# AdaLN attention and FFN in one kernel: the order of the first tiles' statistics on GpSimd and ScalarE, and who splits W_out

## What is computed

```python
mod = (_silu(L0_c) @ L0_wmod).reshape(B, 6, 1, -1)
sa, ca, ga, sb, cb, gb = (mod[:, i] for i in range(6))
ga, gb = ((2 * (g >= 0) - 1) * jnp.maximum(jnp.abs(g), 0.25) for g in (ga, gb))
h = _layernorm(x) * (1 + ca) + sa
x = x + ga * attn(h)      # Xn = layernorm(h)*gamma+beta; Q,K,V = Xn @ W_in + b_in; rotary on K, V
                          # A = 0.5 * sum over rows of cos_sim(K)*cos_sim(V) + 0.5
                          # (A * Q) @ W_out + b_out + h
h = _layernorm(x) * (1 + cb) + sb
x = x + gb * ffn(h)       # relu(h @ W_up.T) @ W_down.T + sum(softmax(top2 logits)) * (h @ W_expert)
```

## Time and profile before

| | us |
|---|---|
| median of 3 executions | 382.82 (381.12 to 384.11) |
| the profiled execution, its own time | 382.15 |
| its span, first to last instruction | 380.1 |
| PE busy in the span | 358.8 (94%) |
| DVE busy | 252.9 (67%) |
| ACT busy | 169.2 (45%) |
| POOL busy | 126.0 (33%) |

### The profile page before, as it was taken

How to read it: one execution, slowest core, us unless ns; L and a number is a source line. 1 busy time by engine, 2 the same in 40 slices (tenths; PEclk the granted TensorE clock), 3 DMA queues, 4 the chain that set the end, 5 groups by cost and what they waited for, 6 DMA issues and landing times.

```text
span 380.1 us, 4613 instructions
## 1 busy us (share of the span) xinstructions
PE 358.8 (94%) x1632; PEld 281.3 (74%) x1632; DVE 252.9 (67%) x510; ACT 169.2 (45%) x307; POOL 126.0 (33%) x127
## 2 busy tenths in 40 slices
PE   4879798999998999989999999999999999999996
PEld 1237286788886888868888878888788878877885
DVE  2788979857978588785988459718550845184354
ACT  1477776773347711375116672156125512541210
POOL 0186746984932439225362142900010001000000
PEclk9989899989999999999999999999999999999999
DMA  6978457430030000000000003001100110011003
GB/s 195 390 310 321 206 223 245 161 93 2 1 83 0 2 0 30 0 1 0 2 28 2 0 0 112 28 0 55 58 3 0 55 57 0 0 59 54 0 2 111
DMA packets 10967, 27.43 MB, mean 72 GB/s; under 512 B 1200, under 2 KB 1584, under 8 KB 9792
## 3 DMA queue, kind: packets, MB, share of 16 engines
q1 hardware_dynamic: 10944, 27.13, 19.7%
HBM read 22.90 MB, written 4.23 MB: 71 GB/s over the span
## 4 chain that ended last, share of the span: by engine, by line
PE 71%; issue 9%; DVE 7%; DMA 4%; ACT 4%; POOL 3%; SPq 1%; DVEq 0%; POOLq 0%; ACTq 0%
PE ps L1144 22%; PE ps L1146 21%; PE ps L1145 21%; DMA stage<-in_wmod 3%; PE ps L1192 2%; DMA xs<-in_X 2%; PE ps L1169 1%; ACT sqj L498 1%; ACT ps L561 1%; POOL hrs L358 1%; POOL w_lo L361 1%; PE ps L1302 1%; PE ps L1303 1%; ACT t_hi L563 1%; DVE hb L735 1%
## 5 line engine op out<-in xcount | busy, mean ns | idle before, releaser
L1144 PE MATMUL ps<-w_hi,t_hi 128*128 128x512 f32 x192 | 76.4, 398 | 0.3 <-POOL w_lo L361 0.3
L1146 PE MATMUL ps<-w_hi,t_lo 128*128 128x512 f32 x192 | 75.5, 393 | 0.0
L1145 PE MATMUL ps<-w_lo,t_hi 128*128 128x512 f32 x192 | 75.3, 392 | 0.0
L1144 PE MATMUL ps<-t_hi,w_hi 128*128 128x512 f32 x128 | 51.2, 400 | 1.4 <-DVE sb_col L1012 1.4
L1144 PE MATMUL ps<-w_hi,g_hi 128*128 128x512 f32 (+1 forms) x132 | 51.3, 389 | 0.0
L1146 PE MATMUL ps<-w_hi,g_lo 128*128 128x512 f32 (+1 forms) x132 | 50.6, 383 | 0.0
L1145 PE MATMUL ps<-w_lo,g_hi 128*128 128x512 f32 (+1 forms) x132 | 50.5, 383 | 0.0
L1146 PE MATMUL ps<-t_hi,w_lo 128*128 128x512 f32 x128 | 50.0, 391 | 0.0
L1145 PE MATMUL ps<-t_lo,w_hi 128*128 128x512 f32 x128 | 49.9, 390 | 0.0
L1144 PEld LDWEIGHTS ps<-w_hi,t_hi 128*128 128x128 f32 x192 | 36.5, 190 | 10.0 <-DVE t_lo L762 1.1
L1146 PEld LDWEIGHTS ps<-w_hi,t_lo 128*128 128x128 f32 x192 | 36.3, 189 | 7.8
(11 more groups left out here) (148 smaller groups left out, 641.4 us busy)
## 6 DMA issues: line engine op xcount, KB each, us to landing
stage<-in_w SPq DMA_DIRECT2D x4, 1024.0 KB, 6.1
out<-xs SPq DMA_DIRECT2D x15, 256.0 KB, 2.0
xs<-in_X SPq DMA_DIRECT2D x3, 1024.0 KB, 9.0
xs<-in_wmod SPq DMA_DIRECT2D x8, 256.0 KB, 6.1
stage<-in_w SPq DMA_DIRECT2D x8, 256.0 KB, 8.5
stage<-in_wmod SPq DMA_DIRECT2D x2, 1024.0 KB, 9.3
gate_bc<-mod_rows SPq DMA_DIRECT2D x8, 256.0 KB, 3.3
xs<-in_X SPq DMA_DIRECT2D x2, 512.0 KB, 6.9
```

The source lines that it names most:

```text
L1144: mm(dst, l_hi, r_hi, start=start, stop=False)
L1145: mm(dst, l_hi, r_lo, start=False, stop=False)
L1146: return mm(dst, l_lo, r_hi, start=False, stop=stop)
```

## The change

On POOL, `rstd_x0(1)` moves behind tile 0's `shift_h0`. On PE, `mod_pair` runs all four chunks ahead of the transposes of tile 0, and the transposes of tile 1 move from before chunk 1 to before chunk 2 of `kv_tile(0,0)`. On ACT, the copy of the scale and shift rows moves from behind the last cast of W_V to a place ahead of tile 0's `t0_evac`, and the cast of W_K's last chunk moves behind tile 1's `normalise`. POOL only casts W_out, four chunks in a row ahead of `rstd_x(2)` and `weight(0,3)`; DVE makes the four low parts behind the last `t_split` of batch 0's turn.

```diff
@@ gpsimd
                 nc.gpsimd.tensor_copy(w_hi[:, WO, k, :], raw).then_inc(whi_out, 1)
-                pool.wait_ge(whi_out, k + 1)
-                nc.gpsimd.tensor_tensor(w_lo[:, WO, k, :], raw, w_hi[:, WO, k, :].bitcast(f32), ALU.subtract).then_inc(wlo_out, 1)
...
                     rstd_h(1, 2, 2)
-                    out_weight(0)
+                    for k in range(NC):
+                        out_weight(k)
                     rstd_x(2)
-                    out_weight(1)
                     weight(b, 3)
-                    out_weight(2)
-                    out_weight(3)
...
             rstd_x0(0)
-            rstd_x0(1)
             low_kv(0, 0)
             shift_h0(0)
+            rstd_x0(1)
             low_kv(1, 0)
@@ scalar
             normalise(0, 0, 1)
             split_hi_kv(1, 2)
-            split_hi_kv(0, 3)
+            act.wait_ge(mod_ps, 1)
+            nc.scalar.activation(rows, ps[0:64, MOD_BANK, :], ACT.Identity, bias=row_bias, scale=half[0:64, 0:1]).then_inc(mod_sb, 1)
             t0_evac(0)
             normalise(0, 1, 1)
+            split_hi_kv(0, 3)
             split_hi_kv(1, 3)
-            act.wait_ge(mod_ps, 1)
-            nc.scalar.activation(rows, ps[0:64, MOD_BANK, :], ACT.Identity, bias=row_bias, scale=half[0:64, 0:1]).then_inc(mod_sb, 1)
             normalise(0, 2, 1)
@@ vector
+            def split_lo_out(k):
+
+                dve.wait_ge(whi_out, k + 1)
+                v.tensor_tensor(w_lo[:, WO, k, :], w_raw[3][:, k * D:(k + 1) * D],
+                                w_hi[:, WO, k, :].bitcast(f32), ALU.subtract).then_inc(wlo_out, 1)
...
                 t_split(1, 2)
                 t_split(1, 3)
+                for k in range(NC):
+                    split_lo_out(k)
@@ tensor
-            def mod_pair(ks):
-                for k in ks:
+            def mod_pair():
+                for k in range(NC):
...
-                if ks[-1] == NC - 1:
-                    last.then_inc(mod_ps, 1)
+                last.then_inc(mod_ps, 1)
...
-                    if b == 0 and t == 0 and k == 1:
+                    if b == 0 and t == 0 and k == 2:
                         transposes0(1)
...
-            mod_pair((0, 1))
+            mod_pair()
             pe.wait_ge(ident_in, 16)
             transposes0(0)
-            mod_pair((2, 3))
```

## The result

The changed kernel takes 387.30 us (median of 4 executions, 386.54 to 388.69), the kernel before 381.97 (4 executions): a ratio on record of 1.0158, 95% interval 1.0093 to 1.0222 (the two medians alone give 1.014). It is slower, by more than the forecast 385.6 and inside the stated range of 380.0 to 388.4. The profiled execution took 387.94 us with a span of 385.8, against 382.15 and 380.1.

What follows compares the result with a forecast made beforehand. The prediction took PE, busy for 94% of the span, to bound the kernel. 0 (parts 1 to 4) + 3.4 (part 5) = 3.4 us on the profiled 382.15 gave 385.6, range 380.0 to 388.4.

Steps and rivals of the forecast that it cites:

- part 5: W_out's subtractions on DVE beside POOL's `base` additions: `q_evac` 5.5 us later, 3.4 lost after cover.
- shared bandwidth: Alternative for DVE's four subtractions beside POOL's additions: about twice 0.645 each, 5.2 us for four, loss under 1.
- Cover: At `out_rows_of(0)`: the fourth chunk is needed three chunks later, which hides 2.05 of the 5.5 us delay.
- 0 to 1.7 more: Low clock behind PE's idling of about 4 us before `out_rows_of(0)`: 0 to 1.7 us of further loss.
- The start: First tiles up to batch 1's transposes: 1.3 us won, 1.8 lost to a clock dip, rounded to 0.
- parts 1 to 4: First tile, `mod_pair` in one go, earlier scale and shift rows, and `a_sums`: together 0 us.
- W_out's casts ahead of `mod_cols`: POOL's four casts hold DVE there: 0.3 us more lost, bounds 1.0 won to 1.4 lost.
- Subtractions cost their own time only: Rival at `ab_col`: no delay beside POOL's additions, 2.0 us won, 380.1, or 378.4 with the start; chance 22%.
- The start keeps its gain: Rival: no clock dip before `kv_tile(0,0)` and Q's chunk 1; 2.7 won against 3.4 lost, 382.9 us; chance 18%.
- further dip: Rival: a clock dip in `out_rows_of(0)`, and casts that hold DVE 1.4 instead of 0.3; 388.4 us; chance 12%.

Runs made afterwards that it cites:

- e8: The changed kernel with four matmuls of no use on PE ahead of the output rows of batch 0; one execution, 385.69 us.
- e1: The changed kernel with W_out's casts and subtractions put back on POOL in their old places; 380.75 us against 380.36 for the kernel before, ratio 1.0019.
- e2: The kernel before with only the W_out part of the change; 384.93 us against 380.36 for the kernel before, ratio 1.0123.
- e9: e6 plus three matmuls of no use ahead of Q's chunk 1 and two ahead of `mod_rest`; 377.55 us against 380.02 for the kernel before, ratio 0.9930.
- e3: The changed kernel with DVE's four W_out subtractions moved up to right behind tile 3's products of K and V; 381.06 us, ratio 1.0017 to the kernel before.
- e10: e3 with the second half of `mod_pair` put back behind tile 0's transposes; 384.36 us, ratio 1.0102 to the kernel before.
- e4: The changed kernel with POOL's eight `base` additions made to wait for DVE's four W_out subtractions; 382.68 us, ratio 1.0063 to the kernel before.
- e6: e3 with five matmuls of no use ahead of the first tile's K and V; 379.41 us, ratio 0.9963 to the kernel before.
- e7: The kernel before with only the W_out part, its subtractions right behind tile 3's products; 380.41 us against 380.38 for the kernel before, ratio 0.9986.
- e5: e3 with five matmuls of no use ahead of the first tile's K and V and five ahead of Q's chunk 1; 380.03 us, ratio 0.9972 to the kernel before.

## Why the prediction was right, and where it was off

- **Sign and place: right.** The loss is made by `split_lo_out` beside `base`, as part 5 said, and by turns rather than shared bandwidth: 6.61 us for the four (7.6 at most was booked, 7.2 with the first wait; sharing would have made 5.2), `ab_col` delayed by one more addition (1.03; alone it takes 0.16, and by sharing it would take about twice that), `q_evac` 4.8 us later within its stage (5.5 booked).
- **Cover: too large by 1.1.** Part 5 took 2.05 off and left the dip at "0 to 1.7 more". 0.9 was covered in the profiled execution; e8, without the dip, covers 15.2 against 17.0, or 1.8. So 0.9 of the difference is the low clock, the term that I had left at 0. The 2.05 itself was also a number of one execution: there the kernel before ran at 0.55 to 0.60 of full clock from 76 to 80 us, so that PE came to `out_rows_of(0)` 8.1 us after `a_sums` began (74.06 to 82.15). In e1, which has W_out as before, the clock stayed up and it came after 6.4 (73.42 to 79.86):

```profile
76.00:78.00 2.00, 2.00 (x10) 1.69 (x9) 0.69 (x1) 1.94 (x4) 2.00 (x3) 1.00 0.28 93
...
79.86 0.39 PE L1150 MATMUL ps<-w_hi,g_hi 128*128 128x512 f32 x1
```

  From `q_evac` to the last addition e1 takes 15.3. So by these two traces 1.65 of the 2.05 was the dip of before, and in an execution of before without that dip almost the whole stall would come through; that fits the medians (4.6 us in e2), but no run singles it out.
- **The start: 0 on the whole, in part by luck, and it scatters.** e1 bears out the sum of parts 1 to 4 (0.2%). In the profiled execution of the changed kernel it lost 1.8: Q's chunk 1 came 0.16 earlier than before instead of 1.3 (62.63 against 62.79), and from there to the transposes the low clock cost 1.95 instead of 1.8. The steps came as told: PE idle from 19.8 to 24.27, the dip in `kv_tile(0,0)`, the rows copied out at 19.41 (26.08 before), `mod_rest` almost without a wait and at full clock, then `mod_cols` late and a second dip. Two sizes were off. DVE's delay was 0.7 at `kv_rows(0,0)` rather than 0.4. And two more of its instructions fell among POOL's low parts of W_Q. Before, and then in the changed kernel:

```profile
45.69 0.28 DVE L788 TENSOR_TENSOR prod<-cross 128x128 f32<-128x128 f32 x1
45.89 0.28 DVE L791 TENSOR_TENSOR prod<-prod 128x128 f32<-128x128 f32 x1
```

```profile
46.39 1.30 DVE L790 TENSOR_TENSOR prod<-cross 128x128 f32<-128x128 f32 x1
47.61 1.38 DVE L793 TENSOR_TENSOR prod<-prod 128x128 f32<-128x128 f32 x1
49.02 1.39 DVE L795 TENSOR_TENSOR prod<-prod,rot_sb 128x256 f32<-128x256 f32 x1
```

  The first two take 0.28 each where POOL is still; the third was held before too (1.38), and L805, held to 2.12 before, now takes 1.01. Net, 1.0 us is lost; with the longer delay that is why Q's chunk 1 came at 62.63 and not at 61.5. Here the same turns worked against the start, which I had not counted. DVE's delay is not what brings it about: in e9, where DVE is ahead of before (`kv_rows(0,0)` at 30.83 against 32.68), the same two are held as long:

```profile
43.86 1.30 DVE L790 TENSOR_TENSOR prod<-cross 128x128 f32<-128x128 f32 x1
45.09 1.37 DVE L793 TENSOR_TENSOR prod<-prod 128x128 f32<-128x128 f32 x1
```

  In the changed kernel, e1 and e9 ACT's cast of W_Q doesn't wait for its DMA (0.78 before), and POOL's low parts begin just ahead of these two (46.25 against 46.39); before, they began only at 45.88, behind the first. In e1 Q's chunk 1 did come at 61.49, the place booked, but by other terms: the same 1.0 lost there, and DVE 0.4 ahead of before at `kv_rows(0,0)` instead of 0.4 behind. That the terms of the start add up to 0 is to that extent luck.
- **W_out's casts ahead of `mod_cols`: right in size.** DVE's instructions there (L793, L795, L758, L807: 0.70, 0.71, 0.56, 1.43 against 0.28, 0.42, 0.15, 1.02 where nothing held them) lost 1.5 us, against 1.3 to POOL before; 0.3 more was booked.
- **The total** was short by 2.3 on the profiled execution (387.94 against 385.6): 1.8 of it the start, 0.5 the stall and its cover (4.8 − 0.9 = 3.9 against 3.4). By medians the loss is 5.3 us, and e2, in another series of executions, shows 4.6 for the W_out part. So the term that was too small is the 3.4 of part 5, by its cover.
- **The rivals.** "Subtractions cost their own time only" fell with e2 and was made true by moving them (e3). "The start keeps its gain" fell in the changed kernel and in e1. With the clock held, e9 is 0.7% faster than before; whether that is the start's gain or the clock's alone is not shown. The "further dip" came, at 0.9.

## What to carry to other kernels

Before an elementwise step is given from one engine to the other of DVE and POOL, look at what the other streams at the place where it lands: with two SBUF inputs it waited here for one instruction of the neighbour per instruction of its own, so 2.5 us became 6.6; the same four lines some 10 us earlier cost nothing. And before a wait is counted as cover, look at whether it stands in every execution: here most of it came from a stretch of low clock. When work ahead of PE is moved earlier, look at where PE then idles: time won in front of an idle stretch can come back as a stretch at 1.2 GHz behind it. An edit that is right needs the other edits that it rests on (e10).

## What the runs showed of the hardware

The scatter from execution to execution goes with the clock. The kernel before varied by 4.9 us in the 25 executions beside e1 to e4 (378.04 to 382.93); e6's executions at a mean clock of 0.990 or 0.991 took 380.0 to 380.3, those at 1.000 377.5 to 378.0; e9, at a mean clock of 0.998 to 1.000, varies by 0.85 us in 12. Whether the clock falls behind a short idle stretch is not the same each time: behind 2.78 us (the kernel before) and 3.24 (e7) at the modulation product it did, behind 3.08 (e2) at the same place it did not, and behind 2.18 (e5) it did while behind 2.12 (e6) it did not. What decides between these was not tried.
